# A one-core attention and mixture-of-adapters block: keys projected first, query products from rounded parts, first group's queries loaded in two pieces

## The reference

```python
x = x + layernorm(attention(layernorm(x), wq, wk, wv, wo))
x = x + layernorm(ffn(layernorm(x), W_base, b_base, W_gate, A, B))
# attention: q, k, v = x @ wq, x @ wk, x @ wv; rotary turn of q and k;
#            softmax(q k^T / 4 + causal mask) v, each key head for 4 query heads; @ wo
# ffn:       x @ W_base^T + b_base + sum over the 2 of 8 experts chosen by softmax(x @ W_gate^T)
#            of weight * (x @ A_e^T) @ B_e^T
```

## Time and profile before

| | |
|---|---|
| median of three runs | 237.78 us |
| the profiled execution, its time | 237.98 us |
| its span | 235.9 us |
| PE busy | 201.3 us (85%) |
| DVE busy | 173.0 us (73%) |
| ACT busy | 134.6 us (57%) |
| POOL busy | 111.1 us (47%) |
| DMA, mean busy share | 44.9% of 16 engines |

### The profile page before, as it was taken

One profiled execution on the slowest core, in us unless ns is written; L12 is line 12 of the kernel. 1 busy time (PEld: TensorE's weight loads), 2 busy tenths in 40 slices (PEclk: granted clock), 3 DMA queues, 4 the chain that ended last, 5 costly groups with the idle time before them and its releaser, 6 DMA issues.

```text
span 235.9 us, 3767 instructions
## 1 busy us (share of the span) xinstructions
PE 201.3 (85%) x1292; PEld 123.1 (52%) x1304; DVE 173.0 (73%) x363; ACT 134.6 (57%) x237; POOL 111.1 (47%) x89
## 2 busy tenths in 40 slices
PE   0599999998878879999999989898789989998760
PEld 0484834434544534545445414146668868997630
DVE  1882617777999796777878791955798898878764
ACT  3340522233043967989766794843467578776970
POOL 8200333553267785889544463744346262442131
PEclk9999999999999999999999999999999999999985
DMA  5998059976977004895940306332410001110113
GB/s 161 388 365 312 4 143 192 254 221 152 192 183 164 14 1 127 181 188 85 199 104 8 53 7 135 62 75 62 90 47 0 3 0 44 46 47 6 38 59 118
DMA packets 22321, 26.73 MB, mean 113 GB/s; under 512 B 3744, under 2 KB 17056, under 8 KB 21536
## 3 DMA queue, kind: packets, MB, share of 16 engines
q1 hardware_dynamic: 22304, 26.51, 44.9%
HBM read 17.19 MB, written 6.95 MB: 102 GB/s over the span
## 4 chain that ended last, share of the span: by engine, by line
PE 50%; DVE 23%; ACT 12%; issue 7%; DMA 3%; SPq 2%; POOL 2%; ACTq 0%; POOLq 0%; DVEq 0%
PE ps L1007 10%; PE ps L1117 7%; PE ps L1102 6%; ACT L558 5%; PE ps L1076 4%; DVE stats L748 4%; PE ps L1017 4%; PE ps L1165 3%; DVE nmax L938 3%; PE ps L993 3%; PE ps L1140 2%; DVE nmax L935 2%; ACT region_a L696 2%; PE ps L1056 2%; PE ps L1071 2%
## 5 line engine op out<-in xcount | busy, mean ns | idle before, releaser
L525 POOL TENSOR_SCALAR_AFFINE_SELECT region_a<-region_a 128x1024 f32<-128x1024 f32 x32 | 37.0, 1157 | 26.9 <-ACT region_a L696 26.6
L938 DVE TENSOR_REDUCE nmax<-ps 128x4 f32<-128x1024 f32 x32 | 39.1, 1223 | 10.3 <-PE ps L1076 10.0
L696 ACT ACTIVATE region_a<-ps 128x1024 f32<-128x1024 f32 x32 | 32.7, 1022 | 0.2 <-PE ps L1102 0.2
L1007 PE MATMUL ps<-region_a,region_c 128*128 128x512 f32 x64 | 29.0, 598 | 0.0
L693 ACT ACTIVATE region_a<-ps 128x512 f32<-128x512 f32 x32 | 19.2, 599 | 16.4 <-PE ps L1102 15.7
L1102 PE MATMUL ps<-region_b,kst 98*128 98x512 bf16 x96 | 26.8, 381 | 1.6 <-ACT region_a L696 1.1
L1117 PE MATMUL ps<-region_a,v_aug 128*32 128x512 f32 x192 | 25.3, 603 | 0.0
L935 DVE TENSOR_REDUCE nmax<-ps 128x4 f32<-128x512 f32 x32 | 21.8, 682 | 4.6 <-PE ps L1060 4.2
L564 ACT ACTIVATE std<-mv,eps_sb 128x1 f32<-128x1 f32 x32 | 9.4, 293 | 26.5 <-DVE mv L749 26.3
L558 ACT ACT_TABLE_LOAD x17 | 21.8, 1283 | 1.1 <-PEq L1261 0.8
L1076 PE MATMUL ps<-kst,region_b 96*128 96x128 bf16 x256 | 19.6, 219 | 1.4 <-DVE nmax L938 0.8
(11 more groups left out here) (104 smaller groups left out, 414.4 us busy)
## 6 DMA issues: line engine op xcount, KB each, us to landing
q_scr<-region_c SPq DMA_DIRECT2D x24, 128.0 KB, 2.5
region_b<-q_scr SPq DMA_DIRECT2D x8, 384.0 KB, 5.0
x_sb<-x SPq DMA_DIRECT2D x8, 256.0 KB, 5.5
region_b<-q_scr SPq DMA_DIRECT2D x8, 256.0 KB, 5.6
attn_t<-o_sb SPq DMA_DIRECT2D x32, 64.0 KB, 2.3
rden_bc<-r_scr SPq DMA_DIRECT2D x8, 256.0 KB, 3.5
out<-region_b SPq DMA_DIRECT2D x8, 256.0 KB, 2.1
kst<-k_scr SPq DMA_DIRECT2D x8, 192.0 KB, 3.7
```

What stands on the lines that cost most here:

```text
L525: pool.affine_select(out=blocks, in_=blocks, compare_op=ALU.is_ge, fill=0.0, base=0, pattern=[[0, 2], [0, REP], [1, P]], channel_multiplie ...
L696: nc.scalar.activation(probs[:, u % PRING, 1:3, :], ps[:, 4:6, :], ACT.Exp, scale=float(HEAD_DIM) ** -0.5).then_inc(exp_done, 1)
L938: nc.vector.tensor_reduce(nmax[:, gi % 2, 1, heads], ps[:, 1:3, :].rearrange("p a (r k) -> p r a k", r=REP), AX.XY, ALU.max, negate=True). ...
L1007: last = nc.tensor.matmul(ps[:, SET_BANKS[i][ri], :], wq_sb[:, c, col:col + P], xn_t[:, c, half * HALF:(half + 1) * HALF], start=(c == 0), ...
```

## The change

1. `SETS` begins with K, then queries (0,0), (0,1), (1,0), (1,1). All eight tiles are turned first. The loads of x tiles 1 and 2 are moved ahead of wv, and wk ahead of wq.
2. Query projections are made of three products of rounded parts (24 matmuls for a set instead of 8). ScalarE rounds x and wq (`high_of_x`, `high_of_wq`), VectorE and GpSimd make the remainders. wq's high part lies where wcat (1296 KB) was loaded, so wcat is loaded at step 9.
3. The i half's addition (before L452) is done by VectorE for the first three sets.
4. K's parts are written once (12 DMAs of 64 KB), the i half's six on ScalarE's queue. `load_k` repeats the parts as it reads: three DMAs with 3, 2 and 1 copies as the outermost dimension.
5. Group 0's queries are loaded in two pieces: the 4 heads of the first unit, then the other 12. `load_q(2)` comes after `load_k(2)`, behind the start of the scores.

```diff
-MATMULS_4 = (1, 1, 1, 1, 1)
+MATMULS_Q = 3 * 2 * KC
+MATMULS_4 = (3, 3, 3, 3, 3)
+WCAT_STEP = 9
...
+        wq_l = over("wq_l", [P, KC, DIM], "region_c", 0)
+        wq_h = over("wq_h", [P, KC, DIM], "wcat_sb", 0)
+        xn_h = over("xn_h", [P, KC, TOKENS], "attn_t", 0)
+        xn_l = [over("xn_l0", [P, KC, HALF], "region_b", 8192), over("xn_l1", [P, KC, HALF], "o_sb", 0)]
...
-        SETS = [(0, 0), "K", (0, 1), (1, 0), (1, 1)]
-        SET_BANKS = [(2, 3), (4, 5), (6, 7), (2, 3), (4, 5)]
+        SETS = ["K", (0, 0), (0, 1), (1, 0), (1, 1)]
+        SET_BANKS = [(2, 3), (4, 5), (0, 1), (6, 7), (4, 5)]
...
+        def write_k(engine, part, ri):
...
+            for half in range(2):
+                dst = k_scr[2 * half:2 * half + 2, part, 8 * ri:8 * ri + 8, :, :].rearrange("b f h n -> (f h) b n")
+                engine.dma_start(dst, parts[half * 64:half * 64 + 64, i % 2, ri, part, :].rearrange("p (b n) -> p b n", b=2))                    .then_inc(k_written[half], 16)
...
+                for part, (first, count) in enumerate(RUNS):
+                    rows = k_scr[b, part, :, g * GROUP_KV:(g + 1) * GROUP_KV, :].rearrange("r h n -> r (h n)")
+                    sp.dma_start(kst[first * HEAD_DIM:(first + count) * HEAD_DIM, gi % RING, :, :],
+                                 rows.unsqueeze(0).broadcast_to([count, HEAD_DIM, GROUP_KV * SEQ]))                        .then_inc(ready or qk_loaded[gi % RING], 16)
...
-            write_q(0)
-            load_q(0)
-            load_q(2)
             for part in range(PARTS):
-                for half in range(2):
-                    write_k(part, half)
-            load_k(0)
+                write_k(sp, part, 0)
+            write_q(1, 0, 1)
+            load_k(0, qk_first)
+            write_q(1, 1, PARTS)
+            load_q(0, slice(0, REP), qk_first)
+            load_q(0, slice(REP, GROUP_HEADS))
             load_k(1)
-            write_q(2)
+            write_q(2, 0, PARTS)
             load_q(1)
             load_k(2)
+            load_q(2)
             load_k(3)
             load_q(3)
-            write_q(3)
+            write_q(3, 0, PARTS)
...
+                if n == WCAT_STEP:
+
+                    sp.wait_ge(proj_psum, len(SETS))
+                    sp.dma_start(wcat_sb[:, :, :], wcat.rearrange("(c p) n -> p c n", p=P)).then_inc(late_loaded, 16)
...
+            low_of_x(pool, 1)
...
+            copy_xnt(TILES - 1)
+            high_of_x(0)
+            high_of_wq(0)
+            high_of_wq(1)
+            high_of_x(1)
             copy_v(0)
...
             split_high(0)
+            write_k(act, 0, 1)
             split_middle(0)
+            write_k(act, 1, 1)
+            write_k(act, 2, 1)
+            split_high(1)
             copy_v(1)
+            split_middle(1)
```

More of the change, by code:

```diff
@@ L196, in build @@
         xnt_ready = sem("xnt_ready")
+        xn_high = sem("xn_high")
+        xn_low = [sem(f"xn_low{i}") for i in range(2)]
+        wq_high = sem("wq_high")
+        wq_low = [sem(f"wq_low{i}") for i in range(2)]
         proj_psum = sem("proj_psum")
@@ L305, in _, with write_q @@
             sp.dma_start(iota_sb[:, :], iota).then_inc(late_loaded, 16)
-            def write_q(i):
+            def write_q(i, first, last):
                 half, g = SETS[i]
                 dst = q_scr[g, 2 * half:2 * half + 2].rearrange("b (s i f) h n -> s i (f h) b n", s=PARTS, i=2)
-                for part in range(PARTS):
+                for part in range(first, last):
                     for ri in range(2):
@@ L322, in write_q @@
                             .then_inc(scr_written[i], 16)
[L324 to L338, removed]
             def wait_ring(gi):
@@ L345, in wait_ring, with load_q @@
                     sp.wait_ge(xnt_psum, TILES)
-            def load_q(gi):
+            def load_q(gi, heads=slice(0, GROUP_HEADS), ready=None):
                 b, g = divmod(gi, 2)
@@ L352, in load_q, with load_k @@
                 for first, count in RUNS:
-                    sp.dma_start(qst[first * HEAD_DIM:(first + count) * HEAD_DIM, gi % RING, :, :],
-                                 q_scr[g, b, 0:count * HEAD_DIM, :, :]).then_inc(qk_loaded[gi % RING], 16)
-            def load_k(gi):
+                    sp.dma_start(qst[first * HEAD_DIM:(first + count) * HEAD_DIM, gi % RING, heads, :],
+                                 q_scr[g, b, 0:count * HEAD_DIM, heads, :]).then_inc(ready or qk_loaded[gi % RING], 16)
+            def load_k(gi, ready=None):
                 b, g = divmod(gi, 2)
@@ L980, in turn_x, with project @@
                 last.then_inc(xnt_psum, 1)
-            def project(i, first=0, count=2 * KC):
-                if i >= 3:
-                    pe.wait_ge(rope_mul, i - 2)
+            def project(i, first=0, count=MATMULS_Q):
+                if i == 4:
+                    pe.wait_ge(rope_mul, 2)
                 if SETS[i] == "K":
@@ L1021, in project_v @@
                     last.then_inc(v_psum, 1)
-            def turn_and_project_v(first):
-                for t in range(first, first + 4):
-                    turn_x(t)
-                    if t > first:
-                        project_v(t - 1)
-                project_v(first + 3)
-            turn_and_project_v(0)
+            for t in range(TILES):
+                turn_x(t)
+                if t >= 1:
+                    project_v(t - 1)
             project(0)
-            turn_and_project_v(4)
-            for i in range(1, 4):
+            project(1)
+            project_v(TILES - 1)
+            for i in range(2, 4):
                 project(i)
-            project(4, 0, 2 * KC - sum(MATMULS_4))
+            project(4, 0, MATMULS_Q - sum(MATMULS_4))
             def scores(n):
@@ L1112, in attend @@
                 pe.wait_ge(probs_masked, 4 * gi + 4)
+                if gi == 0 and piece == 0:
+                    pe.wait_ge(rope_mul, 4)
                 if gi >= 1 and kt == 0:
```

135 lines of the change are left out of this document (92 added, 43 removed).

## The result

The changed kernel took 255.15 us (median of 5 executions, 253.09 to 257.21) against 237.76 (5 executions, 237.44 to 238.17): slower by 6.65%, interval 6.16 to 7.14%. Its executions scatter more than those of before; the ratio leaves its slowest out, the profiled one (256.97 us, span 255.2) among them, so 6.65% is 15.8 us where the two medians differ by 17.4. The forecast of 236.3 and its range to 240.2 are both missed, on the side of the rival in which the maxima land late.

The account below looks back on a forecast made before the run. TensorE, busy 85% of the span, was taken as the bound, then the DMA engines ahead of the first maxima. Head start 5.5 us, 1.5 kept: span 235.9 - 1.5 = 234.4, plus 2.08, less 0.2: 236.3 us, range 232.3 to 240.2.

Parts of the forecast that it names:

- Products: Query projections on TensorE: 24 products a set take 5.8 to 5.9 us against 6.87; TensorE done at 46.1 against 52.8.
- the rival in which they are no faster: Three products at 0.39 us each: 9.4 us a set, TensorE free 5.1 us later, 242.9 us; chance 4%.
- Input tiles: Input stage: x1 lands at about 4.2 us instead of 6.72, and the keys' products can start at 18.3.
- Rounding: Preparing x and wq: VectorE's remainders end between 23.5 and 25.9 us, covered by the keys' products; cost 0, up to 0.6.
- From keys to the first queries: From the keys' parts to the first query load: last low part at 40.5 us, load issued at 43.1.
- a first reduction later than 50: Sign of a wrong forecast: VectorE's first maxima after 50 us, where near 48 was expected against 53.65 before.
- Key loads: Key DMAs on 3 and 2 engines: 2.7 us a group on the two shared engines, against 0.8 spread evenly.
- all 16: Rival: all 16 engines serve the keys, the DMA line ends at 69.3, gain 4.2, 233.6 us; chance 17%.
- DMA line: Busiest engine's transfers up to the first row of maxima, twelve terms: maxima land at 72.0 us, 1.5 gained before scores_t(0).
- the queue doesn't hold the maxima: Rival at the first row of maxima: head start of 5.2 us kept, 232.6 us; chance 10%.
- The slower rival: Maxima land after 73.54, at 75.5 us, through key loads of 3.9 us instead of 2.7; 240.2 us; chance 27%.
- wcat and the second maxima: Second row of maxima behind keys 4, queries 4 and wcat: 9.1 us after the first, needed 9.15 later; no cost.

Follow-up runs that it names:

- a_oldplain: a_oldfix with plain query products instead of three products of rounded parts; ratio 1.0011 to the kernel before.
- c_input: Kernel before with x tiles 1 and 2 loaded first and GpSimd's fill of ones cut in five; ratio 0.9978 to the kernel before.
- a_oldfix: a_oldkeys with GpSimd's long instructions cut and the write of query set (0,1) ahead of group 1's keys; ratio 1.0117 to the kernel before.
- a_oldkeys: Changed kernel with the keys' part undone: written six times, loaded in one DMA a group; ratio 1.0243 to the kernel before.
- b_keys3: Kernel before with the keys' part alone: written once, read in three DMAs of 3, 2 and 1 copies; ratio 1.0427 to the kernel before.
- b_wcat: Kernel before with wcat loaded at step 9 instead of in the input stage; ratio 0.9997 to the kernel before.
- a_keys16: Changed kernel with each group's keys loaded in six DMAs of 16 rows instead of three; ratio 1.0477 to the kernel before.
- c_warm2: c_input with useless products keeping TensorE busy from 2.96 us, ahead of the wait for ident; ratio 0.9896 to the kernel before, 235.33 us.
- a_both: a_keys16 with GpSimd's fill of ones cut in five and its remainder of x's second half in four; ratio 1.0388 to the kernel before.
- a_warm: Changed kernel with useless bf16 products keeping TensorE busy ahead of three waits; ratio 1.0653 to the kernel before.

## Why the prediction was wrong

**Products**: the cost of a set is right, 5.7 us against 5.8 to 5.9, and the rival in which they are no faster falls. The path of TensorE is not. "Q(1,0) 38.1 to 43.9, nine products of (1,1) to 46.1" left out the wait for the second copy of values, taken as "covered by VectorE's work". That copy stands on ScalarE behind the rounding of (0,0)'s queries and came at 43.42, so (1,0) ran from 43.52 to 50.7 and TensorE was free at about 53, 7 late: no sooner than before. With plain products a_oldplain has no such wait (TensorE works from 35.62 to 51.5 without a gap), so the time that the three products save there is mostly waited away.

**Input tiles**: wrong by 2.1 us. "The keys can start at 18.3"; they started at 20.39. The step took for granted that TensorE does a tile in 1.35 us from its beginning and that VectorE's first tile costs 0.55. VectorE's took 2.17 beside the fill of ones, and c_input shows that turning the first tile sooner is worth nothing while the value projections still take 1.92.

**Rounding**: "Cost taken as 0, and up to 0.6 is kept". The cover was counted for TensorE (the keys' products) but not for VectorE, whose last remainder ended at 27.7, not by 25.9, and then met GpSimd's 5.61 us. The first subtraction alone cost 3.1 more (3.79 - 0.69). This cost taken at nothing is one of the steps that failed. a_oldfix against a_oldplain prices preparation less products at 2.5 us net loss.

**From keys to the first queries**: the load forecast at 43.1 came at 50.35, 7.2 late. The last low part was late by 5.5 (46.0 against 40.5): 2.1 from the start and 3.1 from that subtraction. From there to the load it took 4.3 us where 2.6 were forecast. That is the first keys' load, whose three DMAs stand among the writes: without the keys' part (a_oldkeys) it took 1.9 (45.5 to 47.40). The first reduction was at 54.10, forecast near 48: of the head start of 5.5 us nothing was left. Both paths to it ended late: TensorE's products at 53.0, and the queries, for which TensorE then waited 0.68 us more. The text had named a first reduction later than 50 as the sign of its being wrong.

**Key loads**, the main step that failed: the mechanism was right, the size wrong. "3 engines and 2" fits b_keys3's stretches (0.17), but 2.7 us a group was charged as transfer time alone. Three things were missing: the key DMAs hold SP, so that the write behind them is issued 2.8 us late and `load_q(1)` 3.6 in b_keys3; with the queues backed up SP's issues are slow (10.32 us for six, 7.98 in b_keys3); and later loads, taken "at nothing", cost 5.2 us more at group 5 (19.8 against 14.6), 3.6 in b_keys3 and nothing in a_oldkeys. b_keys3 and a_oldkeys put the whole at 10.2 and 10.0 us, where the forecast put 2.7 between few engines and all 16 (236.3 and 233.6). Its "even spread" of 0.8 us is also not what its own rate gives: 192 KB at 396 GB/s are 0.5.

**DMA line**: its shape was right, its sum 5.8 short. From `load_q(1)` to the landing I had 18.4 us (53.6 to 72.0); measured 24.2 (62.27 to 86.5). a_oldfix, without the keys' part, has 56.11 to 76.83, 20.7. That the queue doesn't hold the maxima is refuted by the idle time of 2.88 us ahead of L1173.

**The slower rival** had the right sign, place and mechanism (maxima land after 73.54). Its 75.5 was 11 us early, because it varied only the speed of the key loads and took the head start as given. **wcat and the second maxima**: moving wcat costs nothing by itself, as forecast (b_wcat), but "no cost, and no slack" for the second maxima holds only there: TensorE waited 0.42 us for them in the changed kernel and 1.39 in a_oldplain.

The sign was missed by all of these together, and the keys' part is two thirds of it. The failure is one of bounds: each unknown was bounded by a transfer or an engine's own time, none by what stands behind it in the same queue or on the same port.

## What to carry to other kernels

Before a DMA is made of repeats, look at the outermost dimension on both of its sides: two or three rows there put it on two or three engines here, and what stood behind it came late; the saved writes did not pay for that. Splitting it into more DMAs is no way out if the issuing queue is on the path: twelve issues took 5.77 us of it. Work that is moved to an idle GpSimd is not free for VectorE: cut it in short instructions (3.79 us became 1.73), and count preparation on the engine that has to start the next stage. When an early stage is compressed, sum up what the DMA engines must then carry in the shorter stretch.

## What the runs showed of the hardware

- Issuing slows when engines are behind: the same six writes took 3.26 us (a_keys16), 7.98 (b_keys3) and 10.32 (the change). With the keys' part undone but three query loads in a row it was 5.95 (a_oldfix), so other loads ahead do it in part.
- A GpSimd fill of 2 partitions, 4.36 us long, held up a VectorE instruction of 128 partitions to its own end (2.17 us instead of 0.55); cut in five, the same VectorE instruction took 0.74 (c_warm2) to 0.95 (a_both), and the second tile's up to 1.28 (a_both), since the fill as a whole then lasts 5.13 us.
- GpSimd waits in its turn: its remainder of 1024 columns began at 23.08 beside VectorE's of 22.09 to 24.38 and took 3.53 us, where two of 512 columns at 1.16 would be 2.3; 24.38 + 2.3 is 26.7, and it ended at 26.61.
- TensorE's granted clock fell to 0.50 (1.2 GHz) after idle times of 1.9 to 4.2 us in the changed kernel, but stayed at 1.00 after one of 2.66 us in a_oldfix; where it was lifted (to 76 us and from 86 to 90 in a_warm), the time did not change measurably. At the start the column shows 1.00 while value projections take 1.92 instead of 1.06; products without use from 2.96 us on removed that and brought 1%.
